# Row statistics with one SBUF operand, reciprocals in PSUM, low keys on VectorE, and new orders of work

## What is computed

```python
def reference(x, ctx, mask, Wq, bq, Wk, bk, Wv, bv, Wo, bo, w1, w2):
    q, k, v = heads(layernorm(x) @ Wq + bq), heads(ctx @ Wk + bk), heads(ctx @ Wv + bv)
    scores = where(mask == 0, -1e9, q k^T / sqrt(8))          # [32, 16, 56, 1500]
    x = x + (softmax(scores) v) @ Wo + bo
    xq = quant_act(layernorm(x))      # per row: round(x * 127 / max|x|), clipped, scaled back
    h = gelu(xq @ quant_weight(w1).T)                         # ternary weights, 128 -> 512
    return x + quant_act(h) @ quant_weight(w2).T              # 512 -> 128
```

## Time and profile before

| | us |
|---|---|
| median of 3 runs | 1009.85 (1007.72 to 1011.45) |
| the profiled execution | 1009.53 |
| its span | 1007.8 |
| TensorE (PE) busy | 908.0 (90%) |
| VectorE (DVE) busy | 789.7 (78%) |
| ScalarE (ACT) busy | 675.2 (67%) |
| GpSimd (POOL) busy | 231.7 (23%) |
| mean granted TensorE clock | 0.953 |

### The profile page before, as it was taken

One profiled execution on the slowest core, in us unless ns is written; L12 is line 12 of the kernel. 1 busy time (PEld: TensorE's weight loads), 2 busy tenths in 40 slices (PEclk: granted clock), 3 DMA queues, 4 the chain that ended last, 5 costly groups with the idle time before them and its releaser, 6 DMA issues.

```text
span 1007.8 us, 33628 instructions
## 1 busy us (share of the span) xinstructions
PE 908.0 (90%) x11716; PEld 712.9 (71%) x11716; DVE 789.7 (78%) x2593; ACT 675.2 (67%) x1272; POOL 231.7 (23%) x253
## 2 busy tenths in 40 slices
PE   3767999999999899999999898998989899998983
PEld 2455767777787777777777777877777777877772
DVE  3786778788888778888788878887887888878854
ACT  2444577767768676767777676776777677687661
POOL 6302042221303222220312222130222213032200
PEclk9789999999999899999999999999999999999996
DMA  5520222101222221112222211122221012220000
GB/s 131 114 59 4 56 60 60 49 27 46 55 57 60 57 56 29 45 47 57 60 57 60 51 35 38 52 57 57 60 57 50 28 44 54 57 60 0 4 2 6
DMA packets 59374, 49.34 MB, mean 49 GB/s; under 512 B 2784, under 2 KB 55632, under 8 KB 59344
## 3 DMA queue, kind: packets, MB, share of 16 engines
q1 hardware_dynamic: 57551, 48.11, 18.1%
q10 hardware_dynamic: 1793, 0.83, 0.3%
HBM read 47.91 MB, written 0.92 MB: 48 GB/s over the span
## 4 chain that ended last, share of the span: by engine, by line
issue 66%; POOL 16%; PE 10%; DVE 5%; ACT 2%; DMA 1%; POOLq 1%; DVEq 0%; ACTq 0%
POOL k_lo L574 7%; POOL qry_hi L566 3%; PE ps_p L821 3%; POOL qry_lo L567 3%; PE ps_v L857 2%; PE ps_p L804 2%; DMA ctx_sb<-in_ctx_dram 1%; DVE max_junk L1083 1%; POOL q_lo L564 1%; POOL q_hi L563 1%; PE ps_p L745 1%; ACT probs L660 1%; DVE mask_bias L996 1%; PE ps_p L759 0%; PE ps_p L742 0%
## 5 line engine op out<-in xcount | busy, mean ns | idle before, releaser
L1083 DVE CUSTOM_DVE_ANT_0 max_junk<-ps_p,mask_bias 120x500 bf16<-120x500 f32 x768 | 481.4, 674 | 136.7 <-PE ps_p L804 115.8
L660 ACT ACTIVATE probs<-ps_p 125x448 f32<-125x448 f32 x768 | 359.9, 550 | 94.0 <-PE ps_p L821 88.8
L574 POOL TENSOR_TENSOR k_lo<-k_full,k_hi 128x500 fp32r<-128x500 f32 x96 | 119.9, 1262 | 643.0 <-ACT k_hi L652 638.3
L821 PE MATMUL ps_p<-qry_hi,k_hi 64*125 64x448 f32 x768 | 163.2, 415 | 3.6 <-DVE seg_max L1083 1.7
L804 PE MATMUL ps_p<-k_hi,qry_hi 64*120 64x500 f32 x768 | 151.7, 420 | 13.0 <-POOL qry_hi L566 5.9
L857 PE MATMUL ps_v<-probs,vals 125*32 125x112 f32 x6144 | 162.9, 262 | 0.5 <-ACT probs L660 0.5
L857 PEld LDWEIGHTS ps_v<-probs,vals 125*32 125x32 f32 x6144 | 146.9, 111 | 20.8 <-issue 17.4
L821 PE MATMUL ps_p<-qry_hi,k_lo 64*125 64x448 f32 x768 | 148.1, 375 | 0.0
L642 ACT ACTIVATE k_full<-ps_p,bk_sb 128x500 f32<-128x500 f32 x96 | 64.8, 675 | 122.9 <-PE ps_p L745 122.4
L821 PE MATMUL ps_p<-qry_lo,k_hi 64*125 64x448 f32 x768 | 147.1, 373 | 0.0
L821 PE MATMUL ps_p<-own_query,mask_bias 57*125 57x448 f32 x768 | 147.0, 372 | 0.0
(11 more groups left out here) (124 smaller groups left out, 881.0 us busy)
## 6 DMA issues: line engine op xcount, KB each, us to landing
ctx_sb<-in_ctx_dram SPq DMA_DIRECT2D x31, 750.0 KB
mask_sb<-in_mask_Bx1xSxS_ik_dram SPq DMA_DIRECT2D x64, 328.1 KB
own_query<-shift SPq DMA_DIRECT2D x64, 1.8 KB
out_dram<-x_rows SPq DMA_DIRECT2D x16, 56.0 KB, 1.6
ctx_sb<-in_ctx_dram ACTq DMA_DIRECT2D x1, 750.0 KB
x_rows<-in_x_dram SPq DMA_DIRECT2D x1, 672.0 KB, 10.9
w_sb<-in_L_ffn_w_dram SPq DMA_DIRECT2D x2, 256.0 KB, 8.5
x_rows<-in_x_dram SPq DMA_DIRECT2D x1, 224.0 KB, 6.1
```

The costliest lines, as they stand in the source:

```text
L574: pool.tensor_tensor(k_lo[:, p, at], k_full[:, (p + n) % 2, :], k_hi[:, p, at].bitcast(F32), ALU.subtract)\
L660: act.activation(probs[:, c % NP, h], ps_p[0:KC, BANK[how]["S", c, h], 0:HC], ACT.Exp)\
L821: mm = pe.matmul(ps_p[0:KC, BANK[how]["S", c, h], 0:HC].rearrange("k (a q) -> k a q", a=HH), key[part, :], query[part], start=(n == 0), st ...
L1083: dve.tensor_tensor_reduce(max_junk[0:MROWS, BANK[how][slot], :], ps_p[0:MROWS, BANK[how][slot], 0:SEG], mask_bias[0:MROWS, p, s * SEG:(s ...
```

## The change

`statistics` does the Newton steps for a single tile with `tensor_scalar`, whose second operand is a value per partition, in place of operations on two SBUF tensors; for four tiles nothing changes. The reciprocal of the denominators is written back to the PSUM bank it comes from, and the product reads that bank and `pv_own`; the tile `recip` goes. The low keys are subtracted by VectorE, in slots kl0 to kl2 of its lists, and GpSimd's lists hold q alone. All eight orders are new, and the places of the first pair's additional work on ScalarE with them.

```diff
@@ -62,48 +62,48 @@
 
 
 PE_EVEN = order("""
-    T0 T1 V0 M0 s0 f0 M1 S1 S2 M2 S3 M3 S4 S5 M4 S6 S7 M5 M6 P0 D0 K0 M7 S8 S9 M8 S10 M9 O0 S11 M10 M11 T2 K1 F0
-    V1 V2 K2 R0 P1 P2
+    T0 T1 M0 M1 T2 V0 K0 M2 s0 f0 M3 S1 S2 M4 S3 M5 S4 S5 M6 S6 M7 S7 M8 D0 V1 K1 O0 S8 M9 S9 M10 S10 S11 M11 K2
+    F0 V2 R0 P0 P1 P2
 """)
 
 
 ACT_EVEN = order("""
-    T0 T1 V0 e0 e1 e2 e3 e4 e5 e6 e7 e8 e9 e10 e11 e12 e13 e14 e15 sum0 kf0 e16 e17 e18 e19 e20 e21 e22 kh0 e23
-    T2 kf1 kh1 kf2 V1 V2 kh2
+    sum0 T0 T1 T2 V0 kf0 e0 e1 e2 e3 e4 e5 e6 e7 e8 e9 e10 e11 e12 e13 e14 e15 kf1 V1 e16 e17 e18 e19 kh0 e20
+    kh1 e21 e22 V2 kf2 kh2 e23
 """)
 
 
 DVE_EVEN = order("""
-    own0 m0 m1 m2 m3 m4 m5 m6 m7 m8 m9 bias0 m10 m11 m12 m13 D0 m14 m15 m16 m17 m18 m19 O0 some0 bias1 m20 m21
-    m22 m23 F0 neg0 rows0 R0 rows1 bias2
+    some0 own0 m0 m1 m2 m3 m4 m5 m6 m7 m8 m9 m10 m11 m12 m13 m14 m15 D0 m16 m17 bias0 O0 bias1 m18 m19 m20 m21
+    bias2 m22 m23 neg0 kl0 F0 R0 rows0 kl1 kl2 rows1
 """)
 
 
 POOL_EVEN = order("""
-    kl0 q0 kl1 kl2
+    q0
 """)
 
 
 PE_ODD = order("""
-    V0 T0 H0 s0 M0 f0 S1 S2 M1 S3 S4 M2 M3 G0 P0 M4 S5 M5 S6 S7 M6 S8 S9 M7 S10 S11 M8 M9 P1 P2 M10 M11 K0 U0 V1
-    T1 Y0 T2 D0 K1 F0 K2 R0 V2
+    T0 s0 M0 f0 S1 S2 M1 S3 M2 H0 V0 T1 G0 M3 M4 P0 M5 S4 S5 M6 S6 S7 S8 S9 M7 M8 K0 T2 U0 D0 V1 K1 F0 V2 K2 Y0
+    M9 S10 S11 M10 M11 P1 P2 R0
 """)
 
 
 ACT_ODD = order("""
-    sum0 V0 T0 e0 e1 e2 e3 e4 e5 e6 e7 e8 e9 G0 e10 e11 e12 e13 e14 e15 e16 e17 e18 e19 e20 e21 e22 e23 kf0 kh0
-    T1 V1 T2 kf1 kh1 kf2 V2 kh2
+    sum0 T0 e0 e1 e2 e3 e4 e5 e6 e7 V0 T1 G0 e8 e9 e10 e11 e12 e13 e14 e15 e16 e17 e18 e19 T2 kf0 kh0 kf1 V1 V2
+    kf2 kh1 e20 e21 kh2 e22 e23
 """)
 
 
 DVE_ODD = order("""
-    H0 own0 m0 m1 m2 m3 m4 m5 m6 m7 m8 m9 m10 m11 hid0 m12 m13 bias0 m14 m15 hid1 m16 some0 hid2 hid3 m17 bias1
-    m18 m19 m20 m21 U0 m22 m23 neg0 Y0 bias2 D0 R0 F0
+    m0 m1 own0 m2 m3 m4 H0 m5 bias0 m6 m7 m8 m9 m10 m11 hid0 m12 hid1 m13 hid2 m14 hid3 m15 m16 some0 m17 U0
+    bias1 D0 F0 kl0 Y0 m18 m19 kl1 m20 m21 m22 m23 bias2 neg0 kl2 R0
 """)
 
 
 POOL_ODD = order("""
-    kl0 q0 kl1 kl2
+    q0
 """)
 
 
@@ -140,15 +140,15 @@
 ACT_PASS = passes(
     "T0 T1 T2 X0 kf0 kh0 kf1 kh1 kf2 kh2 sum",
     "T0 T1 T2 sum kf0 kh0 kf1 kh1 kf2 kh2 V0 V1 V2",
-    ACT_EVEN, ACT_ODD, "G0", {"e15": "abs X2", "e5": "X1"}, {"e11": "X3"})
+    ACT_EVEN, ACT_ODD, "G0", {"e11": "X2", "e7": "abs", "kf0": "X1"}, {"T1": "X3"})
 DVE_PASS = passes(
-    "Q0 some F0 bias0 bias1 bias2",
-    " ".join(f"m{n}" for n in range(16)) + " some " + " ".join(f"m{n}" for n in range(16, 21))
-    + " F0 m21 m22 m23 neg R0 bias0 bias1 bias2",
+    "Q0 kl0 kl1 kl2 some F0 bias0 bias1 bias2",
+    " ".join(f"m{n}" for n in range(14)) + " kl0 m14 m15 kl1 some " + " ".join(f"m{n}" for n in range(16, 21))
+    + " kl2 F0 m21 m22 m23 neg R0 bias0 bias1 bias2",
     DVE_EVEN, DVE_ODD, "own D0 O0 rows0 rows1 H0 hid0 hid1 hid2 hid3 U0 Y0",
     {"m1": "norm1", "m7": "norm2", "m9": "Q1", "m11": "B0", "m17": "Q2", "m19": "Z0", "m21": "norm3"},
     {"m7": "W0", "m9": "W1", "m15": "Q3"})
-POOL_PASS = passes("kl0 q0 kl1 kl2", "kl0 q0 kl1 kl2", POOL_EVEN, POOL_ODD, "", {}, {"%s%d" % POOL_ODD[0]: "fold"})
+POOL_PASS = passes("q0", "q0", POOL_EVEN, POOL_ODD, "", {}, {"%s%d" % POOL_ODD[0]: "fold"})
 PREVIOUS = {"lead": "open", "first_even": "lead", "first_odd": "first_even", "even": "odd", "odd": "even",
             "last_even": "odd", "last_odd": "last_even", "tail": "last_odd"}
 
@@ -269,7 +269,6 @@
         shift = sb("shift", [NPAIR, 2, SLOT], F32R)
         probs = sb("probs", [KC, NP, 2, HC])
         pv_own = sb("pv_own", [128, 2, SQ])
-        recip = sb("recip", [128, 2, SQ])
         attn = sb("attn", [128, 2, 2, SQ])
 
         row_n = w1_sb[0:PAIR, 0:1, :]
@@ -566,14 +565,6 @@
                 put_q(pool.tensor_tensor(qry_hi[:, p, :, 0:SQ], head_of_row[:], heads_of(q_hi[:]), ALU.mult))
                 put_q(pool.tensor_tensor(qry_lo[:, p, :, :], head_of_row[:], heads_of(q_lo[:]), ALU.mult))
 
-            def low_keys(bt, n):
-
-                b, k, p = bt
-                at = slice(n * SEG, (n + 1) * SEG)
-                pool.wait_ge(k_hi_ready, NSEG * b + n + 1)
-                pool.tensor_tensor(k_lo[:, p, at], k_full[:, (p + n) % 2, :], k_hi[:, p, at].bitcast(F32), ALU.subtract)\
-                    .then_inc(k_lo_ready, 1)
-
             def fold_bias():
 
                 pool.wait_ge(xn_ready, NGRP)
@@ -586,8 +577,6 @@
                 for kind, n in POOL_PASS[how]:
                     if kind == "q":
                         q_blocks(later(bt, 2))
-                    elif kind == "kl":
-                        low_keys(later(bt, 2), n)
                     else:
                         fold_bias()
 
@@ -909,6 +898,14 @@
                 link(dve.tensor_scalar(bits[:, 9, :], bits[:, 8, :], 1, None, ALU.logical_shift_right))
                 link(dve.tensor_scalar(bits[:, 9, :], bits[:, 9, :], -1.0, RSQRT_BITS, ALU.mult, ALU.add))
 
+                if tiles == 1:
+
+                    for guess, better in ((9, 11), (11, 9), (9, 11)):
+                        link(dve.tensor_scalar(st[:, 10, :], st[:, guess, :], st[:, guess, :], None, ALU.mult))
+                        link(dve.tensor_scalar(st[:, 10, :], st[:, 10, :], st[:, 8, :], -0.5, ALU.mult, ALU.mult))
+                        link(dve.tensor_scalar(st[:, better, :], st[:, 10, :], 1.5, st[:, guess, :],
+                                               ALU.add, ALU.mult))
+                    return
                 for guess, better in ((9, 11), (11, 9), (9, 11)):
                     link(dve.tensor_tensor(st[:, 10, :], st[:, guess, :], st[:, guess, :], ALU.mult))
                     link(dve.scalar_tensor_tensor(out=st[:, 10, :], in0=st[:, 10, :], scalar=-0.5,
@@ -1042,9 +1039,10 @@
 
                     if p == 0:
                         wait(dve, x1_ready, k)
-                    dve.reciprocal(recip[:].rearrange("p t q -> p (t q)"), bank[:, 0:2 * SQ]).then_inc(norm_step, 1)
+                    dve.reciprocal(bank[:, 0:2 * SQ], bank[:, 0:2 * SQ]).then_inc(norm_step, 1)
                     dve.wait_ge(norm_step, b + 1)
-                    dve.tensor_tensor(attn[:, :, p, :], pv_own[:], recip[:], ALU.mult).then_inc(attn_ready, 1)
+                    dve.tensor_tensor(attn[:, :, p, :], bank[:, 0:2 * SQ].rearrange("p (t q) -> p t q", t=2),
+                                      pv_own[:], ALU.mult).then_inc(attn_ready, 1)
                 elif kind == "B":
 
                     dve.tensor_tensor(bo_sb[:], bank[0:PAIR, 0:D], bo_sb[:], ALU.add).then_inc(bo_folded, 1)
@@ -1103,6 +1101,14 @@
                 dve.scalar_tensor_tensor(out=pv_own[:], in0=half[1], scalar=own_half[:, 1:2], in1=pv_own[:],
                                          op0=ALU.mult, op1=ALU.add).then_inc(pv_taken, 1)
 
+            def low_keys(bt, n):
+
+                b, k, p = bt
+                at = slice(n * SEG, (n + 1) * SEG)
+                dve.wait_ge(k_hi_ready, NSEG * b + n + 1)
+                dve.tensor_tensor(k_lo[:, p, at], k_full[:, (p + n) % 2, :], k_hi[:, p, at].bitcast(F32), ALU.subtract)\
+                    .then_inc(k_lo_ready, 1)
+
             def step(st, how):
                 for slot in DVE_PASS[how]:
                     kind, n = slot
@@ -1112,6 +1118,8 @@
                         own_values(later(st, -1))
                     elif kind == "some":
                         find_some(later(st, 2))
+                    elif kind == "kl":
+                        low_keys(later(st, 2), n)
                     elif kind == "neg":
                         turn_max(later(st, 1))
                     elif kind == "bias":
```

## The result

The changed kernel takes 1029.96 us in the median (1028.18 to 1030.36, four runs) where the kernel before takes 1009.18 (1007.72 to 1011.45, four runs): 2.0% slower, the ratio is 1.020 with an interval of 1.018 to 1.022. The whole interval lies above 1; whether the loss is more than 2%, it leaves open. The forecast was 952, with a range of 930 to 984. The sign is wrong, and the size by 78 us.

The account below looks back on a forecast made before the run. TensorE, 90% busy, was taken as the bound, stopped each turn by a 2.4 us wait for VectorE's `shift` and 1.7 us of lower clock. Turn 57.9 to 53.8 us, fourteen turns save 57: 1009.5 - 57 = 952 us, range 930 to 984.

Parts of the forecast that it names:

- part (4): New orders: R0 ahead of `rows0` on VectorE, H0 behind M2; TensorE's matmuls cover the statistics, leaving the 2.4 us stop no place.
- What is late next?: Walk of bank refills in both orders: TensorE's floor 51.5 us a turn, two expected waits of 0.6 us.
- Part (3): Low keys moved to VectorE: GpSimd loses 7.6 us a turn, VectorE gains 3.6, with 3.3 and 7.6 as ends.
- The slower rival: GpSimd's lock delays kl0, kl1 and bias2 ahead of neg0; TensorE waits 3.4 us at R0, clock falls: 1024 us; chance 0.08.
- Part (1): Pointer-scalar statistics on VectorE: nine links of 0.25 us take 2.2 instead of 5.4 us, saving 3.2 a turn, without GpSimd waits.
- Part (2): Reciprocal kept in PSUM: worth nothing in time, bounds 0.1 us a batch either way.
- the statistics don't do what they say: Rival: the statistics' pointer form waits for GpSimd as the old one did; no change, 1009 us; chance 0.05.
- The turn: One loop pass, a pair of batches: 57.9 - 2.4 - 1.7 = 53.8 us, between 52.3 and 56.
- the terms of the stop and its clock: TensorE's wait at V0 for `shift`, 2.4 us, and the lower clock behind it, 1.7 us: 4.1 us a turn.
- the bound of 5 us for the opening and the ends: Opening, first and last pair taken as unchanged: 0, with 5 us either way.
- the small waits: Small waits of TensorE's loads in the present order, making 53.8 us of the 51.5 us floor; new waits cancel against them.
- The rival of 931 us: Tighter packing: clock stays at 1.00, the new order removes small waits too, turn 52.3 us; chance 0.17.

Follow-up runs that it names:

- the kernel with the marks in the loop only: The changed kernel without the 63 semaphore increments in front of row maxima ahead of VectorE's loop, loop untouched: 955.76 us, ratio 0.948 to the kernel before.
- the kernel with 20 ahead: The kernel with the marks in the loop only, low keys back on GpSimd, 20 idle increments starting VectorE's program: 973.51 us, ratio 0.965 to before.

## Why the prediction was wrong

- **The step that failed** is the last of part (4), "What is late next?". It walked the banks of both engines' orders and had no term for VectorE's way back to the loop's start. Part (3) counted six more subtractions as time of VectorE's data path, 3.6 us, and nothing counted the 18 more instructions in the loop as code. The term was put at nothing; it measured 3.9 us of stop at each of 13 returns, and 5.7 us of time. The changed kernel from 300 to 840 us, TensorE's waits and the whole stretch:

```profile
PE ps_p L793 <- DVE seg_max L1081: 22.1, 9, 2.7
PE ps_p L810 <- DVE seg_max L1081: 6.3, 9, 0.7
```

```profile
300.00:840.00 540.00, 508.97 (x6588) 400.79 (x6588) 435.96 (x1455) 382.53 (x716) 58.38 (x74) 0.96 0.18 50
```

  That is 28.4 / 9 = 3.2 us of waits a turn, and a clock of 0.96, worth 2.4 of 60 us: 5.6 together, against the 5.7 measured between the two kernels. The turns themselves are 59.7 and 54.1 us.
- **The slower rival** had the right form (a wait over 2 us, paid again in clock) and nearly the right time, 1024, but by another mechanism and place. That its number is near is luck. The trace shows no lock at kl0 to kl2: all 96 low keys took 658 to 680 ns in the kernel with the marks in the loop only.
- **Part (1) right in its price**: L904, L905 and L906 took 212 to 216 ns each, also beside GpSimd. It was undervalued in its place: alone it is worth 47 us, since it takes 2.4 us of stop and the clock's drop away by itself.
- **Part (2) right**: nothing.
- **Part (3) right in price** (0.67 us busy, VectorE's sum 48.1 a turn against the forecast's 47.9), and without the gain it has: 17.7 us in these orders, for the most part by the end of the lock on `mask_bias`. The forecast knew that row, L996 at 1489 ns, and used it only against the change.
- **Part (4) half right.** "The 2.4 us stop has no place left even if part (1) gave nothing" holds for the whole of the new orders (0.53 and 0.21 us instead), not for R0 ahead of `rows0`, which the text gave as the reason: alone that moves the stop to H0. The rival "the statistics don't do what they say" was therefore mispriced too: 969.5, not 1009.
- **The turn** was forecast as 53.8 and is 54.1 without the stop, so the terms of the stop and its clock were nearly right: 57.9 - 54.1 = 3.8 us against 4.1. Fourteen times these 0.3 us are 4 us, which is all that parts 955.8 from 952; the bound of 5 us for the opening and the ends wasn't needed. Inside the turn two errors cancel. TensorE's work was put at 51.5 and it is busy for 53.8; the small waits, put at some 2, are about 0.25. The rival of 931 us needed a turn of 52.3, below the 53.4 to 53.8 for which TensorE is busy in the two turns at full clock shown above.

## What to carry to other kernels

An edit that adds or takes out instructions of an engine, in its hardware loop or ahead of it, moves the loop against the blocks in which code is fetched. This is shown here for VectorE. Look at the packets of the instruction queue and at the "issue" wait of the loop's first operation before and after, and try the same kernel with some idle instructions ahead of the loop before judging an edit by its time. A stop that leaves one place stands at the next consumer of the same late result, so shorten the chain before reordering around it. What a stop costs depends here on what waits for the engine: 3 us at VectorE's return cost 0.2 to 0.6 us in the old orders, and in the new ones 2.8 and 3.9 us cost 4.1 and 5.7, the lower clock behind TensorE's wait included.

## What was not expected of the hardware

- A shift of VectorE's program by 20 idle instructions changes the time from 1078.7 to 973.5 us, and by 140 against 120 from 958.2 to 1009.3.
- A fetch at the loop's return takes 2.8 to 3.9 us; with the loop's start, by the model, just ahead of an edge there are two, 6.7 us together.
- An operation of VectorE with one SBUF input waits for GpSimd too: `mask_bias`, which took 1.07 us in the row of the kernel with 20 ahead and 417 ns at the median. The prediction had taken from the Trainium skill, "SBUF — State Buffer", section "Who interferes with whom", that one with at most one such input doesn't contend. The prediction left out a condition of the same section: this holds outside the modes that use both pairs of ports, and `tensor_scalar` can run in such a mode, and then contend. By that rule, the trace agrees on the wait; that `mask_bias` ran in such a mode, no run here shows. L904 to L906, also `tensor_scalar`, but on one value a partition, weren't held.
- The lock between VectorE and GpSimd also works the other way round. With the low keys on VectorE, GpSimd's `q_hi` takes 492 ns in the mean where it takes 307 with them on GpSimd, and the low keys' longest on VectorE is 680 ns. The same section says that the order of issue decides who waits. By that rule, the trace agrees: in the loop every `q_hi` that begins inside a low key of VectorE takes 0.67 or 0.68 us, the others 0.30 or 0.31. One pair with the keys on VectorE, then the groups of the two kernels (keys on VectorE, then on GpSimd):

```profile
505.95 0.67 DVE L1110 TENSOR_TENSOR k_lo<-k_full,k_hi 128x500 fp32r<-128x500 f32 x1
506.11 0.67 POOL L562 TENSOR_TENSOR q_hi<-q_flag,ones_f 128x56 fp32r<-128x56 f32 x1 [22.12 <-DVE q_flag L1014]
```

```profile
L562 POOL TENSOR_TENSOR q_hi<-q_flag,ones_f 128x56 fp32r<-128x56 f32 x32 | 15.7, 492 | 735.3 <-DVE q_flag L1014 735.3
```

```profile
L562 POOL TENSOR_TENSOR q_hi<-q_flag,ones_f 128x56 fp32r<-128x56 f32 x32 | 9.8, 307 | 60.2 <-DVE q_flag L1024 60.2
```
